# Passes of layers 0 to 2: four strands of edges side by side, and one input of every wide VectorE operation in PSUM

## The reference

```python
# layer 0: attention over the source's edges
msg = alpha[:, :, None] * xh[row];          out = segment_sum(msg, col, n)      # alpha = exp(..)/sum
# layer 1
msg = edge_weight[:, None] * x[src];        agg = segment_sum(msg, dst, N)
# layer 2: proj is (node, type) -> row
msg = proj[src, edge_type] * attn_mean[:, None];  out = segment_sum(msg, dst, n) + bias
# layer 3: softmax over the target's edges
out = segment_sum(h[src] * alpha[:, None], dst, n) + bias
# after each
x = _layernorm(x + layer(x, ...))
```

## Time and profile before

| | |
|---|---|
| median of 3 runs | 8133.76 us (8036.3 to 8138.81) |
| the profiled execution | 8117.26 us, its span 8115.4 us |
| busy in it: GpSimd (POOL), VectorE (DVE) | 5361.6 us (66%), 3856.3 us (48%) |
| busy in it: TensorE, ScalarE | 894.4 us (11%), 679.1 us (8%) |
| DMA over the span | 770.98 MB, mean 95 GB/s |

### The profile page before, as it was taken

How to read it: one execution, slowest core, us unless ns; L and a number is a source line. 1 busy time by engine, 2 the same in 40 slices (tenths; PEclk the granted TensorE clock), 3 DMA queues, 4 the chain that set the end, 5 groups by cost and what they waited for, 6 DMA issues and landing times. The chain is left out here.

```text
span 8115.4 us, 26187 instructions
## 1 busy us (share of the span) xinstructions
PE 894.4 (11%) x3516; PEld 558.6 (7%) x3516; DVE 3856.3 (48%) x8781; ACT 679.1 (8%) x1577; POOL 5361.6 (66%) x5178
## 2 busy tenths in 40 slices
PE   7500000000000000000025555000000001000000
PEld 5500000000000000000013222000000001000000
DVE  8994454313354343333335665668333334345256
ACT  1021111000000010000013333000000003000002
POOL 0067777767767747777745666666777756767764
PEclk9996555555555555555557877555555555555555
DMA  2081000213333323322225766332332221333332
GB/s 49 1 304 28 2 2 2 57 22 96 87 101 102 91 89 96 95 89 88 93 73 178 250 244 234 101 106 73 96 96 90 92 88 53 82 91 112 83 100 64
DMA packets 275316, 770.98 MB, mean 95 GB/s; under 512 B 122571, under 2 KB 132993, under 8 KB 237129
## 3 DMA queue, kind: packets, MB, share of 16 engines
q0 software_dynamic: 166224, 282.97, 14.7%
q1 hardware_dynamic: 90708, 375.35, 12.8%
q10 hardware_dynamic: 18210, 111.02, 3.6%
HBM read 357.59 MB, written 411.37 MB: 95 GB/s over the span
## 5 line engine op out<-in xcount | busy, mean ns | idle before, releaser
L2172 POOL DMA_INDIRECT l2s_krow<-table_k,l2s_idx x784 | 770.1, 982 | 417.3 <-issue 253.5
L753 POOL DMA_INDIRECT l2z_rows<-proj,l2z_idx x784 | 852.3, 1087 | 254.0 <-issue 238.8
L753 POOL DMA_INDIRECT l3z_rows<-table,l3z_idx x784 | 802.5, 1024 | 304.4 <-issue 237.1
L753 POOL DMA_INDIRECT l1z_rows<-table,l1z_idx x784 | 829.0, 1057 | 263.2 <-issue 239.3
L753 POOL DMA_INDIRECT l0z_rows<-table,l0z_idx x784 | 811.2, 1035 | 285.7 <-issue 239.6
L1707 POOL DMA_INDIRECT first_sj<-scores,first_atdst x784 | 807.1, 1029 | 256.4 <-issue 256.4
L729 DVE SCALAR_TENSOR_TENSOR l1z_acc<-l1z_acc,g_dokeep,l1z_msg 128x128 f32<-128x128 f32 x784 | 278.0, 355 | 569.6 <-DVE l1z_acc L729 379.2
L729 DVE SCALAR_TENSOR_TENSOR l2z_acc<-l2z_acc,g_dokeep,l2z_msg 128x128 f32<-128x128 f32 x784 | 277.8, 354 | 499.1 <-DVE l2z_acc L729 316.0
L729 DVE SCALAR_TENSOR_TENSOR l0z_acc<-l0z_acc,g_dokeep,l0z_msg 128x128 f32<-128x128 f32 x784 | 277.7, 354 | 396.5 <-DVE l0z_acc L729 283.3
L2109 DVE SCALAR_TENSOR_TENSOR l2s_qrow<-l2s_qrow,g_dokeep,l2s_zrow 128x82 f32<-128x82 f32 x1568 | 367.3, 300 | 192.0 <-DVE l2s_qrow L2109 123.1
L2127 PE MATMUL l2s_bank<-l2o_wr,l2s_fed 128*128 128x512 f32 x800 | 415.7, 679 | 301.7 <-ACT l2s_fed L2151 162.0
(11 more groups left out here) (543 smaller groups left out, 3544.4 us busy)
## 6 DMA issues: line engine op xcount, KB each, us to landing
proj<-l2s_proj ACTq DMA_DIRECT2D x100, 1024.0 KB
spread_q<-prep_zero SPq DMA_DIRECT2D x98, 656.0 KB
l2s_zrow<-spread_q SPq DMA_DIRECT2D x98, 656.0 KB
prefix<-l3z_acc SPq DMA_DIRECT2D x48, 1040.0 KB
prefix<-l0z_acc SPq DMA_DIRECT2D x48, 1024.0 KB
prefix<-l1z_acc SPq DMA_DIRECT2D x48, 1024.0 KB
prefix<-l2z_acc SPq DMA_DIRECT2D x48, 1024.0 KB
first_sj<-scores,first_atdst POOLq DMA_INDIRECT x784
```

The lines of the kernel that those rows point to most:

```text
L753: nc.gpsimd.indirect_dma_start(out=rows[:, k % RING, u, :], out_offset=None, in_=table, in_offset=bass.IndirectOffsetOnAxis(ap=idx[:, lo + ...
L2172: nc.gpsimd.indirect_dma_start(out=krow[:, h, u, :], out_offset=None, in_=g.table_k, in_offset=bass.IndirectOffsetOnAxis(ap=idx[:, h, u:u ...
```

## The change

Passes 0, 1 and 2 run through a new `sum_strands`; pass 3 keeps `sum_messages`. The 784 columns of a partition are cut into four strands of 196 (`STRANDS`, `STRIDE`). A turn (`TURNS`, 50 of them as before) takes 4 columns of each strand, so still 16 gathers and 16 rows. The steps are now four per turn, each over the four strands at once (128 x 512), and each is two operations, since one instruction can't take four marks: a product into PSUM (`kept`) and a sum of it with the message. The marks and the weights are copied to PSUM once per pass, so that the weighing, now two operations of 128 x 1024, reads them from PSUM. The store of a turn writes, in each partition, four pieces of 4 rows.

```diff
+STRANDS = 4
+STRIDE = NC // STRANDS
+ABREAST = WIDTH // STRANDS
+def sum_strands(nc, name, g, order, table, prefix, width, weigh, aside):
+        keep, kept = s.ps("keep", [P, STRIDE, STRANDS]), s.ps("kept", [P, STRANDS, D])
+                chain(v.tensor_copy(keep[:], by_step(order.keep[:])))
+                    w.weigh(eng, chain, k, lo, hi)
+                    for u in range(hi - lo):
+                        if lo + u:
+                            eng.wait_ge(summed, lo + u)
+                        here = sums(k)[:, :, u]
+                        chain(v.tensor_tensor(kept[:], last, bc_last(keep[:, lo + u], D), ALU.mult))
+                        v.tensor_tensor(here, kept[:], by_strand(msg[:, 0:STRANDS * (hi - lo)])[:, :, u], ALU.add).then_inc(summed, 1)
+                        last = here
+                v.tensor_copy(g.tail[:], last)
+                out = prefix[0:EP].rearrange("(p c j) f -> p c (j f)", c=STRANDS, j=STRIDE)
+                    sp.dma_start(out[:, :, lo * D:hi * D], sums(k).rearrange("p c u f -> p c (u f)")).then_inc(stored[k % ACCS], 16)
 class Weighed:
-        self.v.tensor_tensor(self.msg[:, 0:n], self.rows[:, k % RING, 0:n, 0:D], bc_last(self.weight[:, lo:hi], D), ALU.mult).then_inc(self.weighed, 1)
+        factor, half = self.factors[:, lo:hi].rearrange("p j c -> p c j"), STRANDS // 2
+        chain.add(self.v.tensor_tensor(msg[:, 0:half], rows[:, 0:half], bc_last3(factor[:, 0:half], D), ALU.mult))
+        self.v.tensor_tensor(msg[:, half:], rows[:, half:], bc_last3(factor[:, half:], D), ALU.mult).then_inc(self.weighed, 1)
 class Attended0(Weighed):
+        self.share = s.ps("share", [P, 2, WIDTH, HEADS])
+        chain(v.tensor_tensor(share, b, rows[:, :, D + 8:D + 12], ALU.mult))
+        chain.add(weigh(slice(0, half)))
+        weigh(slice(half, n)).then_inc(self.weighed, 1)
```

Each partition now has four first runs and four tails. `StrandEnds` (in `source_softmax`, after `row_leads`) finds where they lie: on VectorE two reductions over the 784 marks, four memsets, four scans of 195, four small scalar operations, six small operations and a copy of 128 x 512, with four matmuls. `StrandCompletion` takes the place of `Completion` in the three tails:

```diff
+class StrandCompletion:
+        for c in range(STRANDS):
+            self.nc.gpsimd.indirect_dma_start(out=self.row[:, c, :], out_offset=None, in_=self.prefix,
+                                              in_offset=bass.IndirectOffsetOnAxis(ap=where[:, c:c + 1], axis=0)).then_inc(self.lead, 16)
+        for c in range(STRANDS):
+            pool.wait_ge(self.fixed, c + 1)
+            self.nc.gpsimd.indirect_dma_start(out=self.prefix, out_offset=bass.IndirectOffsetOnAxis(ap=where[:, c:c + 1], axis=0),
+                                              in_=self.row[:, c, :], in_offset=None).then_inc(self.sent, 16)
+        pool.wait_ge(self.sent, 16 * STRANDS)
```

More of the change, by code:

```diff
@@ L647, with __init__ @@
 class Order:
-    def __init__(self, s, name):
+    def __init__(self, s, name, by_strand=False):
         self.keep = s.sb(name + "keep", [P, NC])
@@ new lines, with on_scalar, __init__, __call__ @@
+class Weighed:
+    def on_scalar(self, act, k, n):
+        pass
+    def __init__(self, weight):
+        self.weight = weight
+    def __call__(self, nc, s, us, es, weighed, rows, msg):
+        self.rows, self.msg, self.v, self.weighed = rows, msg, nc.vector, weighed
+        self.factors = s.ps("factors", [P, STRIDE, STRANDS])
+        return self
+    def weigh(self, eng, chain, k, lo, hi):
+        n = STRANDS * (hi - lo)
+        if k == 0:
+            chain(self.v.tensor_copy(self.factors[:], by_step(self.weight)))
+        rows, msg = by_strand(self.rows[:, k % RING, 0:n, 0:D]), by_strand(self.msg[:, 0:n])
+        factor, half = self.factors[:, lo:hi].rearrange("p j c -> p c j"), STRANDS // 2
+        chain.add(self.v.tensor_tensor(msg[:, 0:half], rows[:, 0:half], bc_last3(factor[:, 0:half], D), ALU.mult))
+        self.v.tensor_tensor(msg[:, half:], rows[:, half:], bc_last3(factor[:, half:], D), ALU.mult).then_inc(self.weighed, 1)
+        chain.until()
+        eng.wait_ge(self.weighed, k + 1)
@@ new lines, with __init__, on_vector, on_tensor @@
+class StrandEnds:
+    def __init__(self, nc, s, g, order):
+        self.nc, self.g, self.order = nc, g, order
+        self.run, self.lead, self.own = s.sb("srun", [P, NC]), s.sb("slead", [P, STRANDS]), s.sb("sown", [P, STRANDS])
+        self.full, self.ps = s.sb("sfull", [P, STRANDS]), s.ps("sps", [P, P, STRANDS])
+        self.gone, self.spread = s.sem("sgone"), s.sem("sspread")
+    def on_vector(self, eng, chain):
+        v, g, keep, run, lead, own = self.nc.vector, self.g, self.order.keep[:], self.run, self.lead, self.own
+        v.tensor_reduce(self.full[:], strands(keep, 0, STRIDE), AX, ALU.min).then_inc(self.gone, 1)
+        for c in range(STRANDS):
+            lo, hi = c * STRIDE, (c + 1) * STRIDE
+            chain.add(v.memset(run[:, lo:lo + 1], float(lo)))
+            chain.add(v.tensor_tensor_scan(run[:, lo + 1:hi], keep[:, lo + 1:hi], keep[:, lo + 1:hi], 1.0, ALU.mult, ALU.min))
+            chain.add(v.tensor_scalar(own[:, c:c + 1], g.part[:], float(STRANDS), float(EP + 1 + c), ALU.mult, ALU.add))
+        chain.until()
+        chain(v.tensor_reduce(lead[:], strands(run[:], 0, STRIDE), AX, ALU.add))
+        chain(v.scalar_tensor_tensor(lead[:], g.part[:].to_broadcast([P, STRANDS]), float(NC), lead[:], ALU.mult, ALU.add))
+        chain(v.tensor_tensor(lead[:], lead[:], own[:], ALU.subtract))
+        chain(v.tensor_tensor(lead[:], lead[:], strands(keep, 0, 1)[:, :, 0], ALU.mult))
+        chain(v.tensor_tensor(lead[:], lead[:], own[:], ALU.add))
+        chain(v.tensor_copy(self.order.strand_i[:], lead[:]))
+        eng.wait_ge(self.spread, 1)
+        chain(v.tensor_copy(self.order.strand_full[:], self.ps[:].rearrange("p q c -> p (q c)")))
+    def on_tensor(self, pe):
+        pe.wait_ge(self.gone, 1)
+        for c in range(STRANDS):
+            mm = self.nc.tensor.matmul(self.ps[:, :, c], self.full[:, c:c + 1].to_broadcast([P, P]), self.g.ident[:], start=True, stop=True)
+        mm.then_inc(self.spread, 1)
@@ L1791, in source_softmax @@
         carry = CarryStats(nc, s, g, so, ends)
+        strand_ends = StrandEnds(nc, s, g, O.dst)
         vs, known, named = (s.sem(m) for m in ("vs", "known", "named"))
@@ L1842, in _ @@
                         row_leads(nc, s, "e1", g, O.dst, chain)()
+                        strand_ends.on_vector(eng, chain)
                         eng.wait_ge(loaded[1], 16)
@@ L1896, in layer0 @@
     with Space(nc, "l0r") as q:
-        sum_messages(nc, "l0z", g, O.dst, g.table0, g.prefix, ROW0, Attended0(sj_d), Residual0(nc, q, g, rows, O.dst.some[:]))
+        sum_strands(nc, "l0z", g, O.dst, g.table0, g.prefix, ROW0, Attended0(sj_d[:]), Residual0(nc, q, g, rows, O.dst.some[:]))
     tail0(nc, g, O)
```

195 lines of the change are left out of this document (139 added, 56 removed).

## The result

| | before | after |
|---|---|---|
| median of the runs (5 and 5) | 8111.18 us (8036.3 to 8138.81) | 7994.04 us (7952.43 to 7998.08) |
| the profiled execution | 8117.26 us | 7952.43 us, its span 7950.4 us |
| busy in it: GpSimd, VectorE | 5361.6, 3856.3 us | 5311.1, 3865.4 us |

The ratio is 0.985, with an interval of 0.982 to 0.988. The change gained 1.5%, where 4.7% was forecast (7752 us, range 7670 to 7900).

The account below looks back on a forecast made before the run. GpSimd's gathers were taken to set the pace of passes 0 to 2. From 8117.3, 403.7 saved in the passes and 22.5 added for completion gave 7736; with 16.5 for the median, 7752 us, range 7670 to 7900.

Parts of the forecast that it names:

- The bound of 30 us a pass: Passes 0 to 2: 0.15 us of lengthening might stay on up to a quarter of the gathers; none was charged.
- (b): Gathers lengthened beside VectorE's two-SBUF-input operations: 68.8, 86.6 and 109.9 us in passes 0 to 2, mostly to go.
- (c): GpSimd's waits for a free ring buffer, 35.3 us, in pass 0 alone, forecast to go.
- (d): VectorE's lag behind a pass's last gather, 60.9, 52.1 and 46.2 us, to shrink to 9.6 in pass 0, otherwise 6.6.
- The steps: VectorE's 8 step operations of 512 a turn for 16 of 128, taken at 0.72 us each with hand-off, 5.8 a turn.
- Pass 0 stays slow: Rival, 8%: pass 0's 14 operations step at 1.40 us, a turn takes 23 us, 140 us more than forecast, 7892.
- VectorE becomes the bound: Rival, 5%: product into PSUM and sum out of it cost over 2.3 us each; at 25 us a turn, 8424.
- Completion: Each pass's tail: three more gathers and three more scatters on GpSimd's queue, +7.5 us per tail, 22.5 in all.
- StrandEnds: 20 VectorE operations, 28 us at 1.40 each, charged nothing because VectorE waits for gathers behind them anyway.
- The lengthening stays: Rival, 10%: VectorE's SBUF use as such holds GpSimd at each wide operation; 229.6 us come back, 7982.
- The sign named for it: Gathers beside the new operations taking over 1.1 us would show the forecast wrong in the port.

Follow-up runs that it names:

- g3: Changed kernel without each step's product (6 VectorE operations a turn for 10), in the slow condition: 8036.84 us, kernel before 8105.48.
- c1: The kernel before, unchanged, traced in the quiet condition: 7496.78 us (the group's kernel before 7498.39).
- c2: The changed kernel, unchanged, in the quiet condition: 7349.35 us, kernel before 7498.39, ratio 0.980.
- g1: The changed kernel, unchanged, in the slow condition: 7957.64 us, kernel before 8105.48, ratio 0.982.
- g2: Changed kernel without the stores of the sums in passes 0 to 2, in the slow condition: 7983.30 us, kernel before 8105.48.
- g4: Kernel before with only the weighing's weights (pass 0: its share) moved to PSUM in passes 0 to 2, slow condition: 8133.57 us, kernel before 8105.48.
- c3: Kernel before with only the weighing's weights (pass 0: its share) moved to PSUM in passes 0 to 2, quiet condition: 7350.33 us, kernel before 7498.39.
- h1: Changed kernel without nearly all VectorE work in passes 1 and 2 and without pass 0's steps, quiet condition: 7332.82 us, kernel before 7491.11.
- h2: Changed kernel with five GpSimd fills of 400 columns ahead of each turn's gathers in passes 0 to 2, quiet condition: 7700.86 us, kernel before 7491.11.
- f1: Changed kernel with weights, marks, shares and product all in SBUF, strands kept, quiet condition: 7580.67 us, 1.009 of the kernel before.
- e5: Changed kernel with eight tiny VectorE fills more at the end of every turn of passes 0 to 2, quiet condition: 7345.61 us, kernel before 7500.06.

## Why the prediction was wrong

**The step that failed** is the one on the earlier trace rows: "I take none, because slow stretches go with many short VectorE operations". It put the gathers' share of the slow stretches down to VectorE's short operations, so that fewer of them would end it, and charged nothing. For VectorE's own steps this came true: in passes 0 to 2 of the changed kernel none starts 1.40 us after another. For GpSimd it did not: g3 has 6 VectorE operations for 10, and the turns stay at 22.4 to 22.6 us. The sign was in the row itself: 1.10 us and the gap of 0.30 make 1.40, the spacing of the earlier trace rows, so GpSimd was already at that pace there, and the reduction had no part in it (c1). The bound of 30 us a pass was read off a pass in which the port's lengthening still kept GpSimd's pace near 1.32 us a gather; the passes came out 81, 88 and 79 us above forecast. Freed of the lengthening, GpSimd reaches the slow turns after some eleven turns instead of some 24 and gives the gain back. So (b), valued at 229.6 us, is worth almost nothing in that condition: from the first gather to the last one's end the recorded pair takes 1086.1, 1070.6 and 1091.0 before, 1073.2, 1071.4 and 1086.8 after. That is 16 us in all, with (c)'s 35.3 in it.

**The sum mixed two conditions.** (b) is there to be won in the quiet one and (d) in the slow one; the forecast took both from one trace and added them. In the quiet condition its pass lengths are right: 999.5, 989.5 and 1014.3 forecast; 991.0, 987.8 and 1013.6 in c2, to the last VectorE operation.

Against the forecast's own sum of 7736, the profiled execution of 7952.4 stands 216 us higher. (The medians, 7994 and 7752, lie 242 apart: the profiled execution lies 42 us below its median, where 16.5 was carried over from before.) By its terms:

- The passes, first gather to last VectorE operation: 1080.7, 1077.8 and 1093.1, together 3251.6 for 3003.3, a miss of 248.3. Some 37, 37 and 33 slow turns of 2.4 us more are 257, and the rest came out some 10 us shorter than forecast, as in c2 (2992.4).
- (c), the wait for a ring buffer, is gone, as forecast: the waits of GpSimd name no `msg` operation above 0.3 us. (d) also: VectorE ends 7.5, 6.4 and 6.4 us behind the gathers (9.6 and twice 6.6 forecast).
- The steps: 0.69 us each, as taken from the earlier trace rows for the unseen write to PSUM. No turn of VectorE reaches 20 us. *Pass 0 stays slow* and *VectorE becomes the bound* fall.
- Completion: the chain from first gather to first fetch was 5.69 us and is 13.27 (4053.15 to 4066.42), +7.6 for +7.5. But from a pass's end to the next pass's first gather the recorded pair differs by 23.3, 14.6 and 23.3 us, 61 in all and not 22.5. In the quiet pair it is 27.4. The other 34 us belong to the slow condition. Some 19 of them stand ahead of the completion's first gather, which comes 9.3 to 12.3 us behind the pass's end for 3.9 to 4.4 before, and most of the rest behind the last fetch; what holds the engines there isn't shown.
- StrandEnds at nothing: the first gather of pass 0 comes 10 us earlier in the recorded pair and 8 us later in c2 than in c1; no cost can be told from that scatter.
- Pass 3, left as it was, took 1050.3 us for 1104.2. Its slow stretches were absent in that execution and in g1, but not in g2, g3 and g4, whose pass 3 is the same code. Taken as unchanged, it hid 54 us of the miss, by luck.

The four parts add up: +248.3 + 38.7 (61.2 less the 22.5 of the forecast) - 53.9 - 17 (10 at the start, 7 at the end) = 216.

*The lengthening stays* gave 7982, near the time by the wrong way, and that is luck. A gather beside the new operations takes 0.94 us in the first turns, so it isn't VectorE's use of SBUF that holds it. The sign named for it, gathers over 1.1 us beside the new operations, does appear in slow turns, and there it misled: the same gather, operation and operands take 0.94 at 3152 us and 1.24 at 3414. The comparison with the rule of the Trainium skill (SBUF — State Buffer, Who interferes with whom) stands: c3 shows that a `tensor_tensor` with two SBUF inputs holds the gathers' issue and one with a PSUM input doesn't (21.1 and 20.2 us for sixteen gathers in pass 1, c1 and c3), against the page's inference that descriptor generation isn't held.

**What stays open** is what makes the slow condition. Shown is that it comes and goes between groups of runs, that data are not late, that VectorE's short steps start 1.40 us apart, that GpSimd's mean over a turn settles at 1.40 to 1.41 us a gather in pass 1 with or without the stores and at 6 to 17 VectorE operations, and that this starts after 26 to 29 us have been gained on that pace. Against a plain limit on GpSimd's mean speaks pass 3 of g1, which ran at 21.3 us for sixteen gathers to its end and so gained some 50 us. Pass 0 of g4 doesn't keep the pace either: its turns run from 20.0 to 32.2 us. The tests of it, h1 and h2, met the quiet condition.

## What to carry to other kernels

If GpSimd's queue is the bound, a wide two-input VectorE operation beside its indirect DMAs should have one input in PSUM: one edit, about 1 us for each operation of 2048 elements, and as much as the whole change gained in the quiet condition. In the slow one it gained nothing, so look first at whether the gathers already start 1.40 us apart. Before adding up savings from one trace, ask for each whether it is there in the same condition as the others: a trace taken in the quiet condition would have shown that (c) and (d), some 170 us of the 404, belonged to the other. A stretch whose cause you can't name isn't removed by an edit that merely thins what stands beside it: let one rival price it as staying.

## What the runs showed of the hardware that I had not expected

- The same program takes 7481 to 7534 us or 8036 to 8139 us. Of the 626 us between c1's profiled execution and the recorded one, 28 lie in VectorE's busy time (3828.6 and 3856.3) and 106 in GpSimd's (5255.3 and 5361.6); the rest is busy time of neither.
- VectorE writes a product of 128x512 to PSUM in 0.695 us and reads it back in a sum in 0.691, so an intermediate in PSUM costs it nothing over one in SBUF (0.69 in f1).
- A gather that starts in an operation with two SBUF inputs ends 0.82 us after that operation, whether it lasts 2.25 or 0.69 us (c1 and f1), and what VectorE starts next doesn't hold it. So operations of 0.69 us back to back cost a gather 0.2 us and one of 2.25 costs it 1.0: many short ones are cheaper for it than their total length suggests.
- A fill of 400 columns on GpSimd takes 0.436 us and costs all of it, while eight small VectorE operations a turn (e5) cost nothing.
- The Trainium skill (NOTIFIC — the notification-queue block, 7.1 Overflow: three behaviours, one of which stalls the engine) states that the block that writes the engines' event records can be set to stall the sender of a record while a ring is full. No run here shows whether that is what holds the starts.
